# GpSimd's product of two groups of states with C, walked by pairs of tokens from each group in turn

## What is computed

```
u  = silu(conv3(x));  B, C = split(u @ W_bc + b_bc);  dt = softplus((u @ W_dt + b_dt) @ W_dtp + b_dtp)
h[t] = exp(A * dt[t]) * h[t-1] + B[t] * u[t] * dt[t]          # 128 channels x 16 states
y[t] = sum over the 16 states of C[t] * h[t];   x1 = layernorm(x + y + x * D)
xq = fp4(x1);  hidden = silu(xq @ Wg) * (xq @ Wu);  out = layernorm(x1 + fp4(hidden) @ Wd)
```

## Time and profile before

| | |
|---|---|
| median of 3 runs | 338.46 us (337.42, 338.46, 338.52) |
| span of the profiled execution | 335.0 us |
| median less span | 3.46 us |
| DVE busy | 299.6 us, 89% of the span |
| POOL busy | 264.3 us, 79% |
| PE busy | 262.6 us, 78% |
| ACT busy | 250.8 us, 75% |
| products on GpSimd | 62, 146.7 us busy |

### The profile page before, as it was taken

How to read it: one execution, slowest core, us unless ns; L and a number is a source line. 1 busy time by engine, 2 the same in 40 slices (tenths; PEclk the granted TensorE clock), 3 DMA queues, 4 the chain that set the end, 5 groups by cost and what they waited for, 6 DMA issues and landing times.

```text
span 335.0 us, 4031 instructions
## 1 busy us (share of the span) xinstructions
PE 262.6 (78%) x1172; PEld 129.6 (39%) x1172; DVE 299.6 (89%) x329; ACT 250.8 (75%) x547; POOL 264.3 (79%) x138
## 2 busy tenths in 40 slices
PE   2666976768877897989697969797986779688892
PEld 1222422223322343633353336243542345355592
DVE  3869998999999999999999999999998999986920
ACT  2477889748975788798979887989788577535746
POOL 0075675688459998999999999999999989965840
PEclk9979899799957997999999999999898999999998
DMA  3690662810192009220742055104701000100012
GB/s 44 151 216 8 142 144 63 188 31 0 33 198 53 3 0 201 51 63 0 156 98 64 0 127 126 31 0 97 157 1 31 2 0 0 34 0 0 1 33 63
DMA packets 19261, 21.85 MB, mean 65 GB/s; under 512 B 6112, under 2 KB 15144, under 8 KB 19240
## 3 DMA queue, kind: packets, MB, share of 16 engines
q1 hardware_dynamic: 18520, 21.05, 27.7%
q10 hardware_dynamic: 720, 0.56, 0.9%
HBM read 2.72 MB, written 2.10 MB: 14 GB/s over the span
## 4 chain that ended last, share of the span: by engine, by line
POOL 56%; issue 13%; DVE 11%; ACT 7%; PE 6%; SPq 4%; DMA 2%; DVEq 0%; POOLq 0%; ACTq 0%
POOL product L895 26%; DVE db L1140 5%; POOL hq L945 5%; POOL qh_norm L935 5%; POOL qh_magic L915 5%; POOL qh_norm L910 5%; DVE states L1160 5%; SPq L509 3%; POOL qx_magic L915 2%; POOL qx_norm L910 2%; POOL qx_norm L921 2%; POOL xq L929 2%; ACT ps_decay L565 1%; ACT L555 1%; POOL qh_magic L983 1%
## 5 line engine op out<-in xcount | busy, mean ns | idle before, releaser
L895 POOL TENSOR_TENSOR product<-states,c_rep 128x1024 f32<-128x1024 f32 x59 | 139.4, 2381 | 23.2 <-DVE states L1160 20.3
L565 ACT ACTIVATE ps_decay<-dt_rep,aneg 128x512 f32<-128x512 f32 x128 | 87.0, 691 | 23.3 <-DVE states L1160 15.9
L1160 DVE TENSOR_TENSOR_SCAN states<-ps_decay,db 128x512 f32<-128x512 f32 x64 | 74.9, 1201 | 0.3
L1140 DVE SCALAR_TENSOR_TENSOR db<-ps_b,bbc_rep,dt_rep 128x2048 f32<-128x2048 f32 x31 | 72.1, 2325 | 0.4 <-PE ps_b L1484 0.4
L1160 DVE TENSOR_TENSOR_SCAN states<-ps_decay,states,db 128x512 f32<-128x512 f32 x54 | 66.6, 1260 | 1.0 <-ACT ps_decay L565 1.0
L1484 PE MATMUL ps_b<-u_feat,wbc_rep 128*128 128x512 f32 x64 | 39.1, 695 | 4.7 <-DVE db L1140 4.3
L1478 PE MATMUL ps_prep<-u_feat,wbc_rep 128*128 128x512 f32 x56 | 35.2, 715 | 6.6 <-ACT c_rep L642 6.6
L555 ACT ACT_TABLE_LOAD x26 | 33.4, 1283 | 0.5
L1442 PE MATMUL ps_y<-product,gather 128*32 128x512 f32 x248 | 31.8, 599 | 1.0 <-POOL product L895 1.0
L642 ACT ACTIVATE c_rep<-ps_prep,bbc_rep 128x512 f32<-128x512 f32 x28 | 19.1, 683 | 10.7 <-PE ps_prep L1478 10.7
L1526 PE MATMUL ps_f<-gate_t,xq_t 128*128 128x352 f32 x48 | 17.4, 485 | 8.1 <-ACT hidden L649 6.3
(11 more groups left out here) (250 smaller groups left out, 501.1 us busy)
## 6 DMA issues: line engine op xcount, KB each, us to landing
dt_rep<-dtx SPq DMA_DIRECT2D x124, 128.0 KB, 2.4
x_tok<-in_L_attn_x SPq DMA_DIRECT2D x8, 256.0 KB, 3.0
out<-y_out SPq DMA_DIRECT2D x7, 256.0 KB, 2.3
dt_rep<-dtx ACTq DMA_DIRECT2D x4, 128.0 KB, 3.7
out<-y_out SPq DMA_DIRECT2D x2, 128.0 KB, 1.8
hidden<-in_L_ffn_w_down SPq DMA_DIRECT2D x1, 176.0 KB, 3.4
x_feat<-in_L_attn_x SPq DMA_DIRECT2D x8, 0.5 KB, 2.0
hidden<-in_L_ffn_w_gate SPq DMA_DIRECT2D x1, 128.0 KB, 2.9
```

Source lines behind the costliest of these rows:

```text
L565: nc.scalar.activation(ps_decay[BANK_OF[i]][:], dt_rep[p][:, c, 0, :], ACT.Exp, scale=aneg[:, c, m:m + 1]).then_inc(decay_done, 1)
L895: nc.gpsimd.tensor_tensor(product[:, j % PRODUCTS], groups(s, 2 * j, 2), over(c_rep[p][:, j // SET_PAIRS, :], 2), ALU.mult).then_inc(produ ...
L1140: nc.vector.scalar_tensor_tensor(out=db[m % DB][:], in0=over(ps_b[:], QUADS), scalar=bbc_rep[:, 0, m:m + 1], in1=dt_rep[p][:, :, 1, :], op ...
L1160: nc.vector.tensor_tensor_scan(out=groups(s, k, 1)[:, 0, :], data0=ps_decay[BANK_OF[s.at(GROUPS, k)]][:], data1=db[k // QUADS % DB][:, k % ...
```

## The change

The product's three operands are walked in another order. Before, an instruction goes through 512 tokens of the first group and then through 512 of the second. Now each operand is viewed as 256 pairs of tokens x 2 groups x 2 tokens: two tokens of one group, the same two of the other, then the next two of the first. For C, whose row is the same for both groups, that is c0 c1 c0 c1 c2 c3 c2 c3. The elements computed, the buffers and where each result lies are the same; so are the number of instructions on every engine, their order and their waits. The helper shifts the lines behind it by 5 and the longer call those behind the product by 6, so the product is L895 before and L900 after.

```diff
+def in_turn(t):
+
+    return t.rearrange("p g (t b) -> p t g b", b=2)
...
-                nc.gpsimd.tensor_tensor(product[:, j % PRODUCTS], groups(s, 2 * j, 2),
-                                        over(c_rep[p][:, j // SET_PAIRS, :], 2), ALU.mult).then_inc(product_done, 1)
+                nc.gpsimd.tensor_tensor(in_turn(product[:, j % PRODUCTS]), in_turn(groups(s, 2 * j, 2)),
+                                        in_turn(over(c_rep[p][:, j // SET_PAIRS, :], 2)),
+                                        ALU.mult).then_inc(product_done, 1)
```

## The result

The changed kernel took 334.87 us (334.65 to 335.54, 4 runs) where the kernel before took 338.49 (337.42 to 339.08, 4 runs): ratio 0.990, 95% interval 0.9877 to 0.9923. So it is faster by 2.6 to 3.6 us, where 0.9 was forecast and where 336.7 was the lower end of the range. Three executions in all ran much longer than the others of their kernel (342.5, 629.5 and 855.1 us), and the ratios leave them out.

A forecast was written before the change was run, and what follows sets the result against it. DVE was taken to lead and GpSimd to follow up to 273 us, with GpSimd the bound at the end. Only four last products counted: 338.46 - 0.92 = 337.5 us; 8-in-10 range 336.7 to 347.

The forecast's parts named there:

- The product gets cheaper: GpSimd's 62 products: each 0.23 us less, 2.13 us in place of a median of 2357 ns; chance 0.38.
- these read 6, 4.25, 2.25 and 8 bytes that are new to the instruction: GpSimd's two-input operations: price per element follows new bytes, about 0.10 and 0.115 ns a byte above 4.25.
- The rival that jumps cost: GpSimd's products get dearer through 2 KB jumps after each pair, for example 344.6, 346.8 or 375 us; chance 0.31.
- 44 d - 4.4: Microseconds added if each product costs d more: 6.2 for 0.24, 8.4 for 0.29, 37 for 0.94.
- The floor of some 2.5 cycles an element: Skill page's floor for two-input GpSimd operations, 2.1 ns at 1.2 GHz; the prediction held that the trace disagrees.
- Hidden behind DVE up to 273 us: Units up to 273 us: cheaper products only lengthen GpSimd's waits, from 4.4 to 13.6 us.
- DVE does what it did: DVE in the units up to 273 us: unaffected by GpSimd's cheaper products.
- a change in DVE's durations: Listed sign of a wrong prediction: DVE's own operations change in duration because GpSimd reads in another way.
- The end: From 273.24 us to the end of `hq` at 298.30, GpSimd is the bound; four cheaper products bring 0.92 us.
- 4 x 0.23 = 0.92 us earlier: Last four products, after GpSimd's last wait for DVE at 273.24 us: kernel ends 0.92 us earlier.
- The floor's cap: Rival with products 0.43 us cheaper: end gain limited to PE's 1.37 us idle before `hq`, 337.1 us; chance 0.12.
- The span and what lies around it: Profiled span forecast at 334.1 us, plus 3.46 us around it.

The follow-up runs named there:

- the one run: Kernel before with another row of C for the second group and two tokens in turn, which changes the result: 354.13 us, product 2836 ns.
- the first comparison: Changed kernel against the kernel before, on the first chip: 334.87 us against 338.49, ratio 0.990.
- the second: Changed kernel against the kernel before, timed again on another chip: 335.61 us against 338.24, ratio 0.993.

## Why the prediction was wrong

**The product gets cheaper: right, by another mechanism.** 0.23 was forecast, 0.195 came. The step "these read 6, 4.25, 2.25 and 8 bytes that are new to the instruction" ordered the four rows at hand, but so does the count of meetings (one in 8, 64, 64 and 4 elements), and only the latter holds for the kernels that were built for it. That 0.23 came so close to 0.195 is luck: C with one token in turn (2289 ns) or 8 bytes further (1999 ns) refutes the count that gave it. The rival that jumps cost was weighed at 0.31. It is real where C jumps along with the states (2.84 us), and its price was right: 44 d - 4.4 gives 16.7 us for d = 0.48, and the one run was 15.8 us longer. In this change C stays in its 16 bytes. The floor of some 2.5 cycles an element that the prediction quotes from the Trainium skill (GPSIMD Engine Reference) stands in that page's section 2.1; its section 3.1 says about 2.6. The product of 2.00 us, (2.00 - 0.19) / 1024 = 1.77 ns an element, lies below either.

**Hidden behind DVE up to 273 us: the step that failed.** The prediction says "DVE does what it did", which put the change at nothing up to 273 us, and it was 1.07 us of the 2.1 that separate the two executions below. DVE never waited for GpSimd, and that was read rightly; but a wait inside an instruction is not idle time. It shows as a long duration, and no view of waits lists it. It stood in the profile before: `qh_magic` took 0.77 to 0.93 us in six units and 0.53 in the seventh, when GpSimd stood still. The prediction named a change in DVE's durations among what would make it wrong and gave it no price. The marks of two executions, the kernel before and the one after, taken at DVE's `qx_inv` (98.02, 238.15, 273.66 us before; 97.77, 236.97, 272.34 after), at the end of `hq` (299.15; 297.02) and at the end (335.8; 333.7):

```profile
98.02 0.33 DVE L1088 RECIPROCAL qx_inv<-qx_scale 128x32 f32<-128x32 f32 x1
...
238.15 0.33 DVE L1088 RECIPROCAL qx_inv<-qx_scale 128x32 f32<-128x32 f32 x1
...
273.66 0.33 DVE L1088 RECIPROCAL qx_inv<-qx_scale 128x32 f32<-128x32 f32 x1
```

```profile
97.77 0.33 DVE L1094 RECIPROCAL qx_inv<-qx_scale 128x32 f32<-128x32 f32 x1
...
236.97 0.33 DVE L1094 RECIPROCAL qx_inv<-qx_scale 128x32 f32<-128x32 f32 x1
...
272.34 0.33 DVE L1094 RECIPROCAL qx_inv<-qx_scale 128x32 f32<-128x32 f32 x1
```

```profile
296.56 2.59 POOL L945 TENSOR_TENSOR hq<-qh_magic,qh_scale 128x1408 f32<-128x1408 bf16 x1
```

```profile
294.44 2.58 POOL L951 TENSOR_TENSOR hq<-qh_magic,qh_scale 128x1408 f32<-128x1408 bf16 x1
```

Up to 98 us 0.25 us less, which says nothing: over all kernels this mark lies between 97.6 and 99.0. From there to 273 us 1.07 less, for five `qh_magic` at 0.2; to the end of `hq` 0.81 less; behind it nothing. Together 2.1 us of span, all but the first 0.25 accounted for. The 1.07 is so as a sum and not unit by unit: in the first of the five units DVE's `db` waited 0.19 us longer for PE, which took the gain, and in the third a wait of 0.25 us for ACT was gone.

**The end: right in mechanism and size.** "4 x 0.23 = 0.92 us earlier" measured 0.78 to 0.81. The floor's cap of "at most the 1.37 us that it now idles" was no cap, since DVE's lead moves PE's matmul as well: on the first chip it ends at 296.32 instead of 296.99, and `hq`'s transposes begin 2.14 us sooner (296.22 instead of 298.36).

**The span and what lies around it.** 3.46 us was taken, and about 2 is true of both kernels. This shifted no forecast of the difference, but it hid that the profiled execution was a short one (335.0 us, where twelve others had a median of 336.3). PE's clock may be a part of what makes executions differ. The stretch from 248 to 262 us in the kernel before and in the one with only the last unit changed:

```profile
248.00:262.00 14.00, 9.50 (x34) 4.37 (x30) 12.26 (x12) 10.87 (x22) 13.92 (x8) 0.88 0.07 20
```

```profile
248.00:262.00 14.00, 8.70 (x38) 3.43 (x36) 13.45 (x14) 10.71 (x20) 13.92 (x8) 1.00 0.07 20
```

At a mean granted clock of 0.88 DVE waits 1.09 and 0.65 us for the up matmuls in this stretch (the first is the longest of the earlier trace rows), at 1.00, the higher level throughout, 0.45 us. All four profiles of the kernel before and the changed one have 0.88 here, so this does not tell those two apart. Why the first comparison gave 1 us more than the second is not settled. One piece of it is seen, in a wait that the earlier trace rows leave out; with it DVE waited 3.9 us in all before, and not 3.5:

```profile
DVE db L1140 <- PE ps_b L1484: 0.4, 1, 0.4
```

At 107 us DVE waited 0.41 us for PE's `ps_b` here, 0.59 in the other profile of the kernel before, 0.78 in the changed kernel on the second chip, and not at all on the first. The medians of the changed kernel differ by 0.74 us between the two chips.

## What to carry to other kernels

An engine that never waits may still be held up inside its instructions: compare durations of one instruction over the run, and where they differ look at what the other engines are doing then. Shortening the one instruction that it met was worth as much here as shortening its own. For GpSimd's two-input operations, lay the operands so that they do not come to new 16 bytes at the same element: 8 bytes of offset did more for the product (2.00 us) than a change of order (2.16 and 2.13).

## What the runs showed of the hardware

- GpSimd's product of two float32 rows of 1024 took 2.00, 2.36 or 2.84 us for the same bytes and arithmetic, by how often both operands come to another 16 bytes together (0, 256, 512 times).
- A walk that leaves its row by 2 KB after 8 bytes costs 0.03 us over one that does so after 16, for 256 more jumps, as long as the other operand stays.
- DVE's bfloat16 `qh_magic` and a GpSimd product wait for each other: up to 0.4 us on DVE's side in the kernel before, 0.29 us on GpSimd's. A memset of 0.2 us between two products held DVE up in the same way.
